# Running 13 expert jobs between the stages of the last tiles of a decoder layer

## What is computed

```
x = x + _L0_attn_ref(_layernorm(x, axis=-1), L0_attn_wq, L0_attn_wk, L0_attn_wv, L0_attn_wo, ...)
x = x + _L0_xattn_ref(_layernorm(x, axis=-1), ctx_1024, ctx_1024, mask_Bx1xS2_bk0, L0_xattn_W_out, ...)
x = x + _L0_ffn_ref(_layernorm(x, axis=-1), L0_ffn_ln_gamma, L0_ffn_ln_beta, L0_ffn_router_w, ...)
...
for eid in range(N_EXPERTS):
    xe = xf * dense_gate[:, eid:eid + 1]
    gu = xe @ gate_up_w[eid].T
    gate, up = jnp.split(gu, 2, axis=-1)
    hidden = jax.nn.silu(gate) * up
    out = out + hidden @ down_w[eid].T
```

## Time and profile before

| | us |
|---|---|
| median of 3 runs | 299.69 (299.37 to 300.32) |
| the profiled execution, its time | 298.56 |
| the profiled execution, its span | 296.7 |
| PE busy in the span | 261.5 (88%) |
| DVE, ACT, POOL busy | 195.2, 162.2, 131.2 |

### The profile page before, as it was taken

One profiled execution on the slowest core, in us unless ns is written; L12 is line 12 of the kernel. 1 busy time (PEld: TensorE's weight loads), 2 busy tenths in 40 slices (PEclk: granted clock), 3 DMA queues, 4 the chain that ended last, 5 costly groups with the idle time before them and its releaser, 6 DMA issues.

```text
span 296.7 us, 8959 instructions
## 1 busy us (share of the span) xinstructions
PE 261.5 (88%) x2925; PEld 186.4 (63%) x2926; DVE 195.2 (66%) x793; ACT 162.2 (55%) x345; POOL 131.2 (44%) x186
## 2 busy tenths in 40 slices
PE   7899999999999999999999888576599999999600
PEld 3677788787878878787887654232266666666400
DVE  2767688888889898888988656455144454454416
ACT  2446577657758756765775443100476777777300
POOL 5041333134266356544743734476035565555610
PEclk9999999999999999999999986779999999999955
DMA  7993000000010000000000000013222322322058
GB/s 245 314 424 126 21 1 4 0 6 0 2 32 11 11 22 11 11 23 11 18 12 14 27 11 11 20 39 115 56 63 65 85 74 77 81 66 62 18 157 268
DMA packets 18325, 19.41 MB, mean 65 GB/s; under 512 B 3038, under 2 KB 15073, under 8 KB 17904
## 3 DMA queue, kind: packets, MB, share of 16 engines
q1 hardware_dynamic: 14144, 12.93, 14.6%
q0 software_dynamic: 2272, 4.27, 4.6%
q10 hardware_dynamic: 1872, 1.72, 1.8%
HBM read 12.59 MB, written 6.78 MB: 65 GB/s over the span
## 4 chain that ended last, share of the span: by engine, by line
PE 56%; issue 17%; POOL 13%; DMA 5%; DVE 4%; ACT 2%; POOLq 1%; ACTq 0%; DVEq 0%; SPq 0%
PE quad L435 19%; PE sw_bank L435 12%; PE ko_bank L435 10%; POOL results L1472 8%; PE few_bank L435 4%; PE turn_bank L435 3%; POOL slots L1430 3%; PE quad L518 3%; DMA y_all<-results 2%; PE turn_bank L446 1%; POOL rstd L1374 1%; PE few_bank L556 1%; DMA x_all<-in_x 1%; DVE res_all L1367 1%; DMA slots<-pay,slot_i 1%
## 5 line engine op out<-in xcount | busy, mean ns | idle before, releaser
L1374 POOL TENSOR_TENSOR rstd<-var,cst 128x1 f32<-128x1 f32 (+1 forms) x32 | 26.0, 813 | 92.8 <-DVE var L1054 67.3
L1472 POOL DMA_INDIRECT results<-y_sb,meta x39 | 38.0, 974 | 37.7 <-issue 25.3
L435 PE MATMUL quad<-guT_sb,gT_sb 128*128 x78 | 40.5, 601 | 0.6 <-issue 0.3
L1334 DVE TENSOR_TENSOR hid<-jsilu,quad 128x256 f32<-128x256 f32 x39 | 16.4, 421 | 35.6 <-ACT jsilu L905 31.9
L1430 POOL DMA_INDIRECT slots<-pay,slot_i x32 | 33.1, 1036 | 8.9 <-issue 6.8
L917 ACT ACTIVATE gT_sb<-quad,small_sb 128x128 f32<-128x128 f32 x39 | 17.8, 457 | 19.0 <-PE quad L731 17.1
L905 ACT ACTIVATE jsilu<-quad,g_sb 128x256 f32<-128x256 f32 x39 | 18.5, 474 | 16.3 <-PE quad L435 8.6
L846 ACT ACTIVATE etanh<-quad,xscale 128x1024 f32<-128x1024 f32 x16 | 17.8, 1111 | 5.9 <-PE quad L435 5.9
L435 PEld LDWEIGHTS sw_bank<-wo_sb,oT_sb 128*128 128x128 f32 x128 | 15.5, 191 | 6.4 <-issue 5.7
L435 PE MATMUL sw_bank<-wo_sb,oT_sb 128*128 128x128 f32 x128 | 18.4, 287 | 0.5 <-ACT oT_sb L798 0.5
L798 ACT ACTIVATE v_sb<-quad 128x512 f32<-128x512 f32 x16 | 9.6, 597 | 16.7 <-PE quad L435 16.7
(11 more groups left out here) (141 smaller groups left out, 623.4 us busy)
## 6 DMA issues: line engine op xcount, KB each, us to landing
g_sb<-slots SPq DMA_DIRECT2D x39, 66.0 KB
guT_sb<-in_guT SPq DMA_DIRECT2D x1, 2048.0 KB, 11.9
ctxT_all<-in_ctxT SPq DMA_DIRECT2D x1, 1024.0 KB, 9.6
downT_sb<-in_downT SPq DMA_DIRECT2D x1, 1024.0 KB, 13.9
y_all<-results SPq DMA_DIRECT2D x3, 256.0 KB, 4.6
y_all<-results ACTq DMA_DIRECT2D x3, 256.0 KB, 5.5
out_y<-res_all SPq DMA_DIRECT2D x3, 256.0 KB, 2.7
slots<-tail_sb SPq DMA_DIRECT2D x11, 66.0 KB
```

Of the source, the lines that this page charges most:

```text
L435: return pe.matmul(o, lhsT=l, rhs=r, start=start, stop=stop, **kw)
L1334: nc.vector.tensor_tensor(hid[k][:, :], jsilu[k][:, :], gu_ps[k][:, F:2 * F], ALU.mult).then_inc(hid_ready, 1)
L1374: nc.gpsimd.tensor_tensor(dst, src, half[:, 0:dst.shape[1]], ALU.pow).then_inc(semaphore, 1)
L1472: nc.gpsimd.indirect_dma_start(results, bass.IndirectOffsetOnAxis(meta[kk][:, 1:2].bitcast(I32), 0), y_sb[kk][:, :], None, bounds_check=TO ...
```

## The change

The step loop ends after step 14, and what the engines do from there on is written out as one list for each engine. Into these lists the first 13 jobs are put. They take whole blocks only, blocks that the first ten tiles have filled:

- `count_early` and `early_table`: PE counts the rows of the first ten tiles before rank(10), and DVE runs the same 12 steps on the whole blocks among them, between its other work. `turn_early_table` and `copy_early_table` write the table `early` with 16 lanes, and three more DVE instructions note how many blocks of each expert are taken.
- Jobs 0 to 12 read `early`; SP loads them once the rows of tiles 0 to 9 are in `slots`. Jobs 13 to 38 read the final table, which now has 32 lanes instead of 128 and leaves out the blocks that are taken (two more DVE instructions). Its 12 steps stand between the DVE work of jobs 5 to 8.
- All `keep_warm` calls in the last tiles and around the table are gone; the 15 at the start stay.
- From job 15 on the steps are in the order of before, but written out, with no loop.
- PSUM: three banks for gate_up as before (`sw_bank`, `quad` 0 and 1), one for turn_g (`ko_bank`), and now one each for turn_h (`quad` 3) and for down (`quad` 2), with waits for the reader of the job before (`hT_ready`, `y_ready`).
- `fill_tails` of ACT stands between the ACT work of jobs 8 and 11, that of SP behind the load of job 12. Each of POOL's sends is an item of its list; two of them, of jobs 1 and 2, stand ahead of the last four scatters and ten behind.

```diff
@@
-        gu_ps = [quad[:, 0], quad[:, 1], quad[:, 2]]
-        gT_ps = quad[:, 3, 0:P]
-        hT_ps = [ko_bank, sw_bank]
-        y_ps = [turn_bank[:, 0:D], few_bank[:, 0:D]]
+        gu_ps = [sw_bank, quad[:, 0], quad[:, 1]]
+        gT_ps = ko_bank[:, 0:P]
+        hT_ps = quad[:, 3, 0:F]
+        y_ps = quad[:, 2, 0:D]
...
+            def load_job(j):
+
+                k = j % RING
+                if j == 0:
+                    sp.wait_ge(early_ready, 1)
+                    sp.wait_ge(scattered[0], EARLY_SENT[0])
+                    sp.wait_ge(scattered[1], EARLY_SENT[1])
+                if j == EARLY:
+                    sp.wait_ge(tails_done, 16 * (SPARE + E))
+                    for n in range(2):
+                        sp.wait_ge(scattered[n], 16 * TOPK * NT // 2)
+                    sp.wait_ge(table_ready, 1)
...
-                if i == NT:
-                    keep_warm(6, ko_bank)
...
-            keep_warm(15, quad[:, 1])
...
+            def count_early():
+
+                after(pe, total_ready, EARLY_TILES - 1)
+                after(pe, x2_ready, 12)
+                after(pe, logit_ready, 11)
+                mm(early_count_ps, ones_b, total_b[:, 0], stop=False)
+                mm(early_count_ps, ones_b, total_b[:, 1], start=False)
+
+            def turn_early_table():
+                pe.wait_ge(early_step, TABLE_STEPS)
+                after(pe, x2_ready, 14)
+                for c in range(2):
+                    ins = mm(early_table_ps[:, c * EARLY_LANES:(c + 1) * EARLY_LANES],
+                             jval[:, c:c + 1], ident[:, 0:EARLY_LANES])
+                ins.then_inc(early_done, 1)
...
+            def down(j):
...
+                after(pe, y_ready, j - 1)
                 after(pe, hT_ready, j)
...
+            for i in range(FULL, JOBS + 2):
+                if i + 1 < JOBS:
+                    turn_g(i + 1)
+                if i < JOBS:
+                    gate_up(i)
+                if i - 1 < JOBS:
+                    turn_h(i - 1)
+                down(i - 2)
```

817 lines of the change are left out of this document (658 added, 159 removed).

## The result

The changed kernel takes 291.77 us (median of 4 runs, 290.9 to 292.25) against 300.0 for the kernel before on the same chip (299.37 to 300.82): ratio 0.9717, interval 0.9689 to 0.9744. It is faster, by 8.2 us and not by 20. The profiled execution took 291.36 us, span 289.6; that of before 298.56, so this pair differs by 7.2. The ratios leave out executions over 1.5% above the fastest of the same kernel; the medians do not. Every execution on record, before and after, was recorded by the profiler while it ran.

A forecast was written before the change was run, and what follows sets the result against it. PE bounds the job stage, the last tile's latency the tail. 213.5 + 42.6 + 1.8 + 1.2 + 0.8 = 259.9 for the last down against 279.85, saving 20; median 299.7 - 20.1 = 279.6 us, range 275 to 287.

The forecast's parts named there:

- First early turn, 184.5: In the tail on PE: the early table lets job 0 be turned at some 184.5 us.
- The last row sooner by 2.9 us: Last tile: without two groups of fillings ahead, its normalized row ends near 189.1 instead of 191.56.
- Three gate_up at half clock: PE, ahead of the last tile's turn: three gate_up at 1.7 us each, so the turn is at 192.2.
- choose(14), counts and scatters: Last tile: choose ends 2.2 us late, counts at about 203.5, last scatter lands near 210.1 (208.3 before).
- Final table at 210.1: DVE chain: 3.9 us plus ten job instructions, about 3.6 us, and two steps; ready near 210.1 (205.7 before).
- Job 13 at 213.5: End of the tail: job 13's first turn at about 213.5, 2.7 us later than the old job start, 210.84.
- ten sends to make up at 1.28 us each: Job stage: 0.8 us added for POOL's ten sends and for ACT standing behind by its 3 us.
- 26 jobs at 1.64 with no loop: Job stage on PE: 26 jobs take 42.6 us; the loop had added 0.05 us a job.
- What costs nothing: Job stage: one PSUM bank each for turn_h and down is free; lost cover would cost 2.6 us per 0.1.
- the stretching tail: Rival: late job instructions stop the last tile at four places, tail 6.6 us longer still, 286; chance 0.14 in all.
- The dearer table switch: Rival on ACT: each new table load costs 1.28 us more on the path, 282; 0.03 within the 0.14.
- the losing rival: Rival: without fillings the job stage runs at half clock, 44 us slower, 344; chance 0.02.

The follow-up runs named there:

- set 1: The changed kernel as it is against the kernel before on the same chip: 291.77 us, ratio 0.9717.
- set 2: Three variants of the changed kernel (282.89, 288.17, 287.48 us) and the kernel before with its loop written out (294.17), against the kernel before, 296.21 us.
- table_unmixed: Changed kernel with the final table's twelve DVE steps in one run, without the nine job instructions between them: 287.48 us, ratio 0.9721.
- the sends: Changed kernel with POOL's sends of jobs 1 and 2 moved behind the last four scatters: 288.17 us, ratio 0.9735.
- 42 fillings: Changed kernel with 42 keep_warm matmuls put back on PE in the tail: 282.89 us, 0.9566 in set 2; 294.39 us, 0.9831 in a later set.
- sets 1, 3, 4 and 5: Sets of the changed kernel and its variants, each against the kernel before on the same chip; plain changed kernel 291.77, 292.38 and 292.64 us, none in the third of these.
- set 6: Changed kernel with POOL pauses, 42 fillings and late expert load: 288.11 us, 0.9583; also with early table, all tails from SP, 32 fillings: 288.67 us, 0.9630.
- the pauses: Changed kernel with POOL copies of about 0.75 us put between indirect DMAs of the tail: 290.06 us, ratio 0.9688; with 42 fillings too, 289.5 us, 0.9664.

## Why the prediction was right in direction and wrong in time

The direction and the mechanism held: work moved under the last tiles' latency is saved. The time, 291.8, is outside the range of 275 to 287. Held against its own steps, by the trace of set 1:

- *First early turn, 184.5:* came at 184.87. The early table is no problem.
- *The last row sooner by 2.9 us because two groups of fillings are gone (189.1):* wrong. It ended at 192.53, 3.4 us late, having started at 192.19. Without fillings alone it starts at 192.14 in the kernel before, and with fillings put back, in set 2, at 188.36, where the table_unmixed kernel without them has 190.87. What I took off as PE time was given back by half clock and by waits.
- *Three gate_up at half clock (3.1 us from row to turn):* 2.9, though one of the three had run before the row was there. Routing and exponential likewise: 2.2 and 0.9 us further, forecast 2.1 and 1.3. A table load costs nothing on the path: it hides ahead of the logits.
- *choose(14), counts and scatters:* both_b at 203.81, 2.4 us later than forecast, no worse than the exponential; the counts then 4.3 us late, about 2.2 of it the second late stretch (2.5 us from rank(14) to `place`, 0.3 in set 2).
- *Final table at 210.1, "ten instructions of jobs, about 3.6 us":* 219.1. This is the step that failed. I priced the jobs' instructions by their durations, and not what they wait for: scale(4) 1.84 us and scale(5) 3.42 us, the latter behind PE's third late signal. Of the 9.0 us, 4.3 are the late counts and 4.7 the chain: it took 11.1 us from the copy of the counts, where I had 6.4. Even in set 2, with fillings and without late signals, it takes 9.1. As the sends show, a send may stand in the same place. The sum was wrong too: 203.7 for the copy, 3.9 for the chain and 3.6 for the jobs are 211.2 and not 210.1.
- *Job 13 at 213.5:* 224.39, 10.9 late. Nine of it are the table's; the rest is that I let job 13 wait for its load alone (3.4 us behind the table), while PE's own list between the two takes 5.3 us, part of it at half clock (218.8 to 222.2). With no late signals and the clock low for 3.4 us only (42 fillings, set 2) it is at 215.8, 2.3 late. So most of the 10.9 goes with these two, as far as sets on different chips can be compared; how much is due to each is not shown. The second is the clock: at its lower level, 1.2 GHz, for 23.9 us of the tail in set 1 (13.7 before). They hide each other: fillings alone gain nothing where signals are late (227.9); where they aren't, job 13 stands at 219.9 without fillings and with the table unmixed, and at 215.8 with fillings and the table mixed.
- *POOL: "ten sends to make up at 1.28 us each", 0.8 us:* the mechanism was wrong. POOL was not late; its run of DMAs held up the signals of PE. The trace of before had it already, and it is on the last tile's way there: PE ended tile 15's sums at 185.24, and DVE starts on them 2.0 us later. The same lists in set 2 (with the loop written out) have 0.05 us between the two. So the kernel before pays for it as well, which is part of why it takes 3 to 4 us less in set 2.

```profile
184.13 1.11 PE L435 MATMUL quad<-vcb,ex_sb 128*64 128x18 f32 x32
...
187.29 0.26 DVE L1027 RECIPROCAL rden<-quad 128x16 f32<-128x16 f32 x1 [2.61 <-remote]
```

And set 2:

```profile
182.16 1.11 PE L435 MATMUL quad<-vcb,ex_sb 128*64 128x18 f32 x32
...
183.32 0.26 DVE L1027 RECIPROCAL rden<-quad 128x16 f32<-128x16 f32 x1 [0.63 <-PE quad L435]
```

- *26 jobs at 1.64 with no loop:* the loop's share was right (1.9 us measured). The written-out jobs of this kernel take 1.716, 1.8 us more over 24 jobs. `turn_g` loads the expert's number ahead of gate_up; behind it most jobs take 1.64, but only 0.9 us of the 1.8 came in the stage. The order of that one load I had not priced. "What costs nothing" held for the single banks where the signals are on time; behind a late one PE waited 0.41 us for the scale of the job before.

Sum of the misses at the last down: 10.9 + 1.8 + about 0.7 behind job 13 that I can't place are the 13.4 us between its forecast end, 259.9, and its end at 273.3. Of the rivals, the stretching tail was the one that happened, 6 us beyond its number. The dearer table switch is excluded: the load starts at 197.18, takes 1.28 us, and the exponential starts at 198.47, 0.01 us behind it. The Trainium skill's 2.66 us for a switch (ScalarE: Activation LUTs, What ACT_TABLE_LOAD costs) does not appear in this trace. The clock came back in the job stage (1.00), so the losing rival had no part.

Open: what makes a set one of late signals. Every run of three DMAs 1.3 us apart at the first turn had them in sets 1, 3, 4 and 5, and none in set 2. The chip was the same in sets 2 and 6, and in set 6 signals are late at the counts (2.2 and 1.2 us) in spite of the pauses. That pauses in POOL's run take delays away is shown; what the signals wait for is not, nor why the issuing of tails by SP and ACT stands still with them. One rival is untested: the recording itself, which every timed execution had and which loses update records in the same sets. Whether the signals are late in an execution that is not recorded, nobody measured.

## What to carry to other kernels

When work moves into a stretch where an engine was idle, price what each moved instruction waits for at its new place in the list, and not its duration alone. Look in the trace for engines that start long after their releaser ended, under a run of indirect DMAs, and look in the trace of before too: the baseline may pay for it already. And where cures for two causes hide each other, try them together, on one chip, with the unchanged version beside them; a single edit that does its own part and leaves the time alone is not yet a reason to drop it.

## What the runs showed of the hardware that I had not expected

- Under a run of POOL's indirect DMAs 1.3 us apart, what PE ended reaches ACT and DVE late in four sets out of five (set 6 has only kernels with pauses): 2.4 to 2.5 us at the first turn (3.4 with fillings), 2.3 to 2.5 at rank(14), 1.1 and 2.0 in the two traces with the lists of before. Several signals arrive at once, 1.6 to 1.8 us after the run's last DMA started. With the DMAs 1.55 us apart it is 0.05 to 0.6 us at the first turn.
- In the longest of these stretches SP and ACT issue their DMAs late too: SP's four tails take 7.25 us in set 1, 2.83 in set 2.
- The same sets lack records of semaphore updates of PE where the waiting engine started 0.04 us after PE ended.
- The same kernel before takes 296.2 us in the set without this and 299.2 to 300.5 in the others.
- A register load on PE between a transpose and the matmul whose address needs it goes with 0.07 us more a job (1.716 against 1.64 with the load behind the matmul), though only 0.9 of 1.8 us was gained over the stage.
